# A graph-network layer on one NeuronCore: offset table laid out in slots of 16 words, norm statistics made one tile ahead

## The reference

```python
agg_edge = jax.ops.segment_sum(edge_attr, dst, num_segments=12500)   # 12500 x 48
h = jnp.maximum(_layernorm(x, axis=-1), 0.0)                         # 12500 x 128
collected = jnp.concatenate([h, agg_edge], axis=1)                   # 12500 x 176
y = jax.nn.silu(collected @ W1 + b1)                                 # 176 -> 256
y = jax.nn.silu(y @ W2 + b2)                                         # 256 -> 256
return x + h + (y @ W3 + b3)                                         # 256 -> 128
```

## Time and profile before

| | us |
|---|---|
| median of 3 runs | 417.44 (416.64 to 420.57) |
| the profiled execution | 418.25 |
| its span in the trace | 416.5 |

### The profile page before, as it was taken

The page is one execution under the profiler, slowest core; times in us unless marked ns, Lnnn a source line. Parts: engine busy times, 40 slices in busy tenths (PEclk is TensorE's granted clock), DMA queues, the critical chain, the costliest instruction groups (busy, mean ns, idle before and its releaser), DMA issues.

```text
span 416.5 us, 13441 instructions
## 1 busy us (share of the span) xinstructions
PE 331.1 (80%) x5150; PEld 300.3 (72%) x5151; DVE 267.1 (64%) x634; ACT 213.9 (51%) x406; POOL 60.8 (15%) x44
## 2 busy tenths in 40 slices
PE   6556777977797779877897779777977798778885
PEld 6445777966687668866787669666966787677875
DVE  7954558566766686668656766667566765785443
ACT  7643446346644564455544653456346644465372
POOL 2101011012211222022202220122012110110000
PEclk9967969999999999999999999999999999999999
DMA  7970524633664256533663356435632675340101
GB/s 215 290 216 2 155 58 124 178 105 84 169 176 132 82 138 176 160 89 104 176 171 91 94 172 176 107 82 164 176 106 77 171 179 147 101 121 24 44 22 43
DMA packets 79194, 53.07 MB, mean 127 GB/s; under 512 B 2912, under 2 KB 78778, under 8 KB 79168
## 3 DMA queue, kind: packets, MB, share of 16 engines
q1 hardware_dynamic: 79168, 52.70, 46.1%
HBM read 46.29 MB, written 6.40 MB: 127 GB/s over the span
## 4 chain that ended last, share of the span: by engine, by line
PE 40%; issue 21%; DMA 20%; DVE 13%; ACT 3%; SPq 2%; DVEq 0%; POOL 0%; ACTq 0%; POOLq 0%
DMA x_t<-in_x_dram 20%; PE stage L919 16%; PE z L997 6%; DVE onehot L632 6%; PE agg_ps L936 4%; DVE stats L606 3%; PE z L982 3%; PE z L986 2%; PE z L983 2%; SPq L297 2%; DVE meanvar L612 2%; PE tp L949 1%; PE z L965 1%; PE z L970 1%; PE z L971 1%
## 5 line engine op out<-in xcount | busy, mean ns | idle before, releaser
L919 PE MATMUL stage<-onehot,raw 128*48 128x42 f32 x3128 | 81.8, 221 | 61.7 <-issue 60.8
L919 PEld LDWEIGHTS stage<-onehot,raw 128*48 128x48 f32 x3128 | 78.7, 132 | 71.4 <-issue 71.3
L403 POOL TENSOR_TENSOR rstd<-vareps,minus_half 112x4 f32<-112x4 f32 (+1 forms) x28 | 57.6, 2059 | 334.9 <-DVE vareps L616 334.9
L632 DVE TENSOR_TENSOR onehot<-window,rel 128x1176 f32<-128x1176 f32 (+1 forms) x56 | 76.9, 1375 | 2.7 <-ACT rel L433 1.3
L805 DVE TENSOR_TENSOR out_t<-z,resid 112x512 f32<-112x512 f32 (+1 forms) x28 | 19.4, 691 | 71.3 <-PE z L997 71.3
L997 PE MATMUL z<-w,h 128*112 128x128 f32 (+1 forms) x448 | 56.2, 278 | 0.9 <-ACT h L491 0.8
L997 PEld LDWEIGHTS z<-w,h 128*112 128x112 f32 (+1 forms) x448 | 50.8, 177 | 2.7 <-issue 1.4
L441 ACT ACTIVATE staged<-stage 112x294 f32<-112x294 f32 x28 | 11.6, 416 | 68.4 <-PE stage L919 68.4
L936 PE MATMUL agg_ps<-staged,ident 112*48 112x42 f32 x782 | 42.5, 219 | 5.1 <-issue 5.1
L470 ACT ACTIVATE xn<-x_t,nmr,rstd 112x128 f32<-112x128 f32 (+1 forms) x112 | 45.9, 480 | 0.1
L936 PEld LDWEIGHTS agg_ps<-staged,ident 112*48 112x48 f32 x782 | 39.2, 129 | 9.2 <-issue 5.7
(11 more groups left out here) (108 smaller groups left out, 415.9 us busy)
## 6 DMA issues: line engine op xcount, KB each, us to landing
raw<-in_edge_attr_dram SPq DMA_DIRECT2D x55, 672.0 KB, 6.2
x_t<-in_x_dram SPq DMA_DIRECT2D x27, 224.0 KB, 5.3
out_dram<-out_t SPq DMA_DIRECT2D x27, 224.0 KB, 4.6
dst_rows<-in_dst_dram SPq DMA_DIRECT2D x1, 512.0 KB
raw<-in_edge_attr_dram SPq DMA_DIRECT2D x1, 480.0 KB, 5.8
dst_rows<-in_dst_dram SPq DMA_DIRECT2D x1, 256.0 KB, 2.7
out_t<-in_L_gnn_W_dram SPq DMA_DIRECT2D x1, 256.0 KB, 8.2
x_t<-in_x_dram SPq DMA_DIRECT2D x1, 192.0 KB
```

Source lines behind the costliest of these rows:

```text
L403: pool.tensor_tensor(rstd[0:np_, parity], vareps[0:np_, :], minus_half[0:np_, :], ALU.pow).then_inc(s_rstd, 1)
L632: return dve.tensor_tensor(onehot[:, slot, 0:n * PER, :], window[:, :].unsqueeze(1).broadcast_to([P, n * PER, WINDOW]), cols.unsqueeze(2). ...
L919: mm = pe.matmul(stage[at:at + ED, pair * WINDOW:(pair + 1) * WINDOW], raw[0:rows, 2 * parity + half, k, j, :], onehot[0:rows, 2 * parity ...
```

## The change

It has three parts.

1. **The offset table.** `offset_row` gets NT slots of SLOT = 16 words. Batch b now begins at word 16b and has its 14 words there without a gap; two words of a slot stay unused. Batch 0 has its 11 words at word 3, batch 27 its 16 words at word 432. Counted from the beginning of `offset_row`, the words where a 14-word batch begins were 11, 25, 39, ... (all odd) and are now 16, 32, 48, .... VectorE fills the table with six copies in place of two. `offset_row` itself begins at the same address in both kernels.
2. **Norm statistics one tile ahead.** In step i VectorE handles `load_stats`, `aggregate_stats` and `shift_of_norm` of tile i+1 where it handled those of tile i, and GpSimd `rstd_of(i + 1)`. Tile 1's are made in the prologue. VectorE's order within a step is rewritten.
3. **SyncE's order.** In a step: x of tile i+1, edges of tile i+3 (both halves), store of tile i-2.

```diff
-        offset_row = sb("offset_row", [1, ROWS * P], I32)
+        offset_row = sb("offset_row", [1, NT * SLOT], I32)
...
             def step(i, parity):
-                if has(i, -3, NT):
-                    load_edges(i + 3, 1 - parity, 0)
                 if has(i, -1, NT):
                     load_x(i + 1, 1 - parity)
-                if has(i, -3, NT):
-                    load_edges(i + 3, 1 - parity, 1)
+                for half in range(2):
+                    if has(i, -3, NT):
+                        load_edges(i + 3, 1 - parity, half)
                 if has(i, 2, NT):
                     store(i - 2, parity)
...
-                if has(i, 0, NT):
-                    rstd_of(i, parity)
+                if has(i, -1, NT):
+                    rstd_of(i + 1, 1 - parity)
...
             rstd_of(0, 0)
             pool.iota(tile_i[:, :], pattern=[[1, TILE]], base=0, channel_multiplier=0).then_inc(s_pool_zero, 1)
+            rstd_of(1, 1)
...
-            dve.tensor_copy(offset_row[:, 0:P], z3[0:1, 0, :]).then_inc(s_off0, 1)
+            place_row = z3[0:1, :, :].rearrange("p q d -> p (q d)")
+
+            def offsets_into(b, first, last, many=1):
+                g0 = b * GPT - EARLY + first
+                into = offset_row[:, b * SLOT:(b + many) * SLOT].rearrange("p (b k) -> p b k", k=SLOT)[:, :, first:last]
+                return dve.tensor_copy(into, place_row[:, g0:g0 + many * (last - first)].rearrange(
+                    "p (b k) -> p b k", b=many))
+
+            FULL0 = (P + EARLY) // GPT
+            REST0 = (P + EARLY) % GPT
+            offsets_into(0, EARLY, GPT)
+            offsets_into(1, 0, GPT, FULL0 - 1)
+            offsets_into(FULL0, 0, REST0).then_inc(s_off0, 1)
...
-            dve.tensor_copy(offset_row[:, P:], z3[0:1, 1:ROWS, :].rearrange("p q d -> p (q d)"))
+            offsets_into(FULL0, REST0, GPT)
+            offsets_into(FULL0 + 1, 0, GPT, NT - 2 - FULL0)
+            offsets_into(NT - 1, 0, NG + EARLY - (NT - 1) * GPT)
             dve.tensor_reduce(any_invalid[:, :], invalid_sum, AX.X, ALU.max).then_inc(s_off, 1)
             weights_lo()
             dve.wait_ge(s_rel, ROWS)
+            load_stats(1, 1)
+            dve.wait_ge(s_stats, 2)
+            aggregate_stats(1, 1)
             for half in range(2):
                 make_onehot(2, 0, half)
+            shift_of_norm(1, 1)
...
-                    offset_row[0:1, bass.ds(b * GPT + first, last - first)], engines=[mybir.EngineType.PE],
+                    offset_row[0:1, bass.ds(b * SLOT + (first + EARLY), last - first)], engines=[mybir.EngineType.PE],
```

More of the change, by code:

```diff
@@ L65, in gnn_kernel @@
     assert N * GROUP == NPG * E and E % PER == 0 and N % PER == 0
+    SLOT = 16
     PAIRS = GPT // 2
@@ L809, in step @@
                 if has(i, 1, NT):
+                    add_x(i - 1, 1 - parity)
+                    carry_over(i - 1, 1 - parity)
                     relu_lo(i - 1)
[L811 to L815, removed]
                     agg_lo(i - 1)
-                if has(i, 0, NT):
-                    aggregate_stats(i, parity)
                 if has(i, -2, NT):
                     make_onehot(i + 2, parity, 0)
-                if has(i, 0, NT):
-                    shift_of_norm(i, parity)
+                if has(i, -1, NT):
+                    load_stats(i + 1, 1 - parity)
+                    dve.wait_ge(s_stats, i + 2)
+                if has(i, 1, NT):
+                    add_b3(i - 1, 1 - parity)
+                if has(i, -1, NT):
+                    aggregate_stats(i + 1, 1 - parity)
                 if has(i, 1, NT):
                     h1_lo_part(i - 1, 0)
-                    add_x(i - 1, 1 - parity)
                     h1_lo_part(i - 1, 1)
@@ L828, in step @@
                     make_onehot(i + 2, parity, 1)
-                if has(i, 1, NT):
-                    add_b3(i - 1, 1 - parity)
+                if has(i, -1, NT):
+                    shift_of_norm(i + 1, 1 - parity)
                 if has(i, 2, NT):
```

## The result

The changed kernel takes 359.66 us in the median (358.91 to 360.5, 4 runs), the kernel before 418.63 in the same comparison: a ratio of 0.859 (95% interval 0.854 to 0.864). The forecast was 374.0 with a range of 368 to 388. The direction and the mechanism were right, the size was not: the gain is 59 us where 43.5 were forecast.

The account below looks back on a forecast made before the run. TensorE was taken as the bound, with gaps from its sequencer's register load: 418.25 - 41.0 (gaps) - 0.45 (prologue) - 2.1 (`agg_hilo` wait) = 374.7 us, less 0.8 to the median, rounded to 374; range 368 to 388.

Parts of the forecast that it names:

- The bound: TensorE: 26 gaps before `sum_tile`, 60.8 us in all, ended by its own sequencer's load of the offsets, 3.34 us in the median.
- The load's new duration: TensorE's offset loads: 14 words fetched in pairs from an even start take 1.77 us, 1.57 less; 41.0 us saved in all.
- blocks of four: Alternative reading of the offset load: words fetched four at a time, 368 ns a block, 1655 ns for 14 words.
- Rival E: TensorE's clock, at half speed in stretches of the first 85 us: a few us either way, inside the range; no separate chance.
- The prologue: TensorE's 5.06 us wait before its first placement, with both first offset loads in it: 0.45 us less.
- The wait for `agg_hilo`: TensorE standing still at the start when x comes late: 2.1 us less, since x leaves that chain.
- Part 2's ring: VectorE and the x load: 6.6 us plus x's landing of 4 us, 10.6 against a period of 11.98; costed at nothing.
- Nothing gained, nothing lost: SyncE's new order: edges go out two periods before they are needed and no later wait holds them; 0 us.
- B: Offset loads: the layout does nothing, the period stays 13.55 us and only 2.1 us go: 415.3 us; chance 0.06.
- A: Offset loads get shorter by less, 2.22 us with blocks of eight: 386 us; chance 0.06 for loads clearly over 1.9.
- C: The ring through VectorE becomes the bound: x lands after 6 us, period 12.6 us, time 391 us; chance 0.08.
- D: Slower: the ring through VectorE with x landing after 7.5 us, period 14.1 us, time 429 us; chance 0.03.

Follow-up runs that it names:

- e1: The kernel before with the new offset table alone, statistics and SyncE's order as before: 363.3 us, ratio 0.862.
- e2: The changed kernel with the old offset table, keeping the statistics one tile ahead and SyncE's new order: 415.0 us, ratio 0.983.
- e6: The changed kernel with batch 0 at word 0 of its slot and batch 1's load issued first: 356.9 us in a single run.
- e3: The changed kernel with a table without gaps, moved by three words, so batch b begins at word 14b: 397.64 us, ratio 0.942.
- e1b: The kernel before with the new offset table and SyncE's new order, statistics as before: 359.63 us, ratio 0.858.
- e7: The changed kernel reading whole 16-word slots, from batch 2 on in two loads of 8 words, before `sum_tile` and before `place_batch`: 346.22 us, ratio 0.826.
- e5: The changed kernel with every load reading all 16 words of its slot: 351.38 us, ratio 0.839.

## Why the prediction was wrong

**The bound** was read rightly: the register load in TensorE's sequencer, seen as "issue" in front of `sum_tile`. e1 and e2 show it from both sides.

**The load's new duration is the step that failed.** The forecast put it as "If words are fetched two at a time where they begin at an even word" and took 1.77 us, with a bound of 1655 ns for blocks of four; measured were 1.34. Both numbers came from one row, batch 0's 1520 ns, and that row had 0.19 us in it which every first load pays (e6). Without it (batch 0's words took 1324 ns in e6) the forecast's own working gives 1.49 us for 14 words by pairs and 1.36 by blocks of four; the blocks are the reading that fits, and e3 rules out pairs. With the numbers of the runs: 16 words are four blocks, (1106 - 87) / 4 = 255 ns a block; 8 words, (594 - 87) / 2 = 254; 14 words are three blocks and two singles, 3 x 255 + 2 x 232 + 87 = 1316, measured 1340. So a load saves 2.00 us, the last one 2.69, and in the gaps 60.8 - 9.1 = 51.7 us were saved where 41.0 were forecast: 10.7 of the 15.8 us that the profiled execution lies below its forecast of 374.7. It would have been 53 but for the unrolled steps, where the gap was only some 1.8 to 2.2 us and up to 0.2 is left.

**Rival E, the clock, was mis-sized as a side matter.** TensorE's busy time fell by 4.9 us (331.1 to 326.2), nearly all of it in `sum_tile`, which ran at half speed less often at the start, and never after it (in the kernel before once more, at 290.5). The forecast had "a few us to either side" in the range and nothing in the sum.

**The prologue** gained 0.28 us (5.06 to 4.78) where 0.45 was said. **The wait for `agg_hilo`** went wholly, 2.8 us, where 2.1 was said; the forecast put it down to part 2, but e1b shows that part 3 takes it away without part 2. The sum of what was found is 51.7 + 4.9 + 0.3 + 2.8 = 59.7 us, against 418.25 - 358.91 = 59.3.

**Part 2's ring** was rightly costed at nothing for this kernel: x lands in 3.5 us in the median, where "4 us" was estimated, and VectorE kept 1.56 us of waiting. But the sentence on part 3, "Nothing gained, nothing lost", is wrong twice. On top of the table alone, part 3 takes away the wait for `agg_hilo`: 3.4 us of e1, whose span is 3.0 us longer than e1b's. And part 2 without part 3 would have cost 196 us. The forecast weighed x only at the place that the changed code gives it, and did not ask which part of the change put it there.

**The rivals.** B, the layout does nothing, fell with the first row of loads. The Trainium skill's rule of about 200 ns per register even in bulk ("Runtime: NRT & Kernel Launch", instruction fetch mechanics) holds here only for words that are fetched singly: 232 ns each. For blocks of four it is off by a factor of three, 255 ns for four registers. The page says nothing of where a load begins; "whatever its address" was the forecast's reading of it. A, C and D did not happen.

The range broke at its lower end because that end was set by the lowest bound of one reading of one row, 1655 ns, and that row was the least typical of its kind.

## What to carry to other kernels

When an engine's wait ends on "issue", look at its sequencer: a load of run-time values into registers can stand in front of the work at 232 ns a word. Lay such words out so that each load begins on a multiple of four words and reads a multiple of four, and cut the load so that each piece is shorter than the work already queued in front of it; here that, together with SyncE's new order, took some 72 us out of 419. When one duration carries an estimate, ask first whether it is a first execution, and leave room beyond its bounds.

## What the runs showed of the hardware

- The register loads of this case fit a line: 87 ns, and 232 ns for each word fetched singly (1 word 319 ns, 14 words 3336, 16 words 3800). Where the load begins on a multiple of four words, each full group of four costs about 255 ns (8 words 594 ns, 16 words 1106). A load that begins elsewhere gains nothing, even where aligned groups lie inside it (3336 ns for all 14-word loads before, 3350 at a start of two more than a multiple of four).
- Reading more can be quicker: 16 words 1106 ns, 14 words 1340.
- The first such load of the program costs about 0.19 us more (1300 against 1106, 1527 against 1340).
- A register load of 0.6 us between groups of matmuls costs no time on the array (e7: busy 100.00 of 100 us); one of 1.1 us leaves a gap of 0.2 us (e5).
- Behind idle gaps of 1.8 to 2.7 us before `sum_tile` the clock fell to half in six of the 11 slow steps of e3 after its first 85 us, and in one of 23 steps of the kernel before; what tells the two apart was not tried.
